# Two experts' halves of a shared K-tile as 64-row matmuls side by side, with outputs rotating over three PSUM banks

## The reference

```
hmid = gelu(einsum('tc,ech->eth', xf, w1) + b1, approximate=True)   # 4 experts, 576 hidden
eo = einsum('eth,ehc->etc', hmid, w2) + b2
moe = einsum('te,etc->tc', cw, eo)                                  # cw: top 2 of 4, softmax
x = x + g_mlp * moe
```

## Time and profile before

| | us |
|---|---|
| median of 3 runs | 472.41 |
| lowest and highest | 471.92, 477.0 |
| the profiled execution | 469.73 |
| its span, first to last instruction | 467.9 |
| PE busy | 416.6 |
| DVE, ACT, POOL busy | 281.4, 270.9, 129.5 |

### The profile page before, as it was taken

The page is one execution under the profiler, slowest core; times in us unless marked ns, Lnnn a source line. Parts: engine busy times, 40 slices in busy tenths (PEclk is TensorE's granted clock), DMA queues, the critical chain, the costliest instruction groups (busy, mean ns, idle before and its releaser), DMA issues.

```text
span 467.9 us, 10745 instructions
## 1 busy us (share of the span) xinstructions
PE 416.6 (89%) x4010; PEld 337.7 (72%) x4010; DVE 281.4 (60%) x797; ACT 270.9 (58%) x515; POOL 129.5 (28%) x214
## 2 busy tenths in 40 slices
PE   3784689898899999999998999998899998999997
PEld 1353568586676689878976897798678676768885
DVE  7965577687964426258623663257776657774642
ACT  4543277986596580382067336813677766777662
POOL 3104034352212072036008300714142432121000
PEclk9976599999999999999999999999799999999999
DMA  7955555546444000100010205203336465210212
GB/s 210 194 131 159 143 159 144 150 128 162 156 116 125 20 1 2 27 0 1 0 27 1 56 23 162 91 2 78 102 109 176 155 150 177 75 42 1 52 50 77
DMA packets 51570, 42.51 MB, mean 91 GB/s; under 512 B 33595, under 2 KB 43762, under 8 KB 51514
## 3 DMA queue, kind: packets, MB, share of 16 engines
q1 hardware_dynamic: 51450, 41.80, 32.7%
q10 hardware_dynamic: 68, 0.02, 0.0%
HBM read 33.20 MB, written 8.29 MB: 89 GB/s over the span
## 4 chain that ended last, share of the span: by engine, by line
PE 56%; DVE 13%; ACT 10%; SPq 7%; issue 6%; DMA 5%; POOL 3%; DVEq 0%; ACTq 0%; POOLq 0%
PE bank L1687 14%; PE bank L1705 4%; PE s_pair L1525 3%; PE bank L1567 3%; PE st_pair L1548 3%; DVE mx L1258 3%; PE s_pair L1465 2%; SPq L692 2%; PE s_pair L1472 2%; PE s_pair L1466 2%; PE s_pair L1469 2%; PE st_pair L1465 2%; PE bank L1458 2%; DMA hid<-mT 2%; PE st_pair L1466 2%
## 5 line engine op out<-in xcount | busy, mean ns | idle before, releaser
L1258 DVE TENSOR_REDUCE mx<-s_pair 128x8 f32<-128x1024 f32 x62 | 75.7, 1221 | 37.5 <-PE s_pair L1525 37.0
L961 ACT ACTIVATE pr<-st_pair 128x1024 f32<-128x1024 f32 x64 | 65.6, 1025 | 27.7 <-PE st_pair L1548 27.4
L1687 PE MATMUL bank<-w_sb,hid 128*128 128x144 f32 x640 | 80.5, 287 | 1.0 <-DVE aT L1337 1.0
L1687 PEld LDWEIGHTS bank<-w_sb,hid 128*128 128x128 f32 x640 | 79.6, 190 | 1.8 <-DVE aT L1337 1.2
L1010 ACT ACTIVATE hid<-s_pair 128x512 f32<-128x512 f32 x40 | 23.3, 612 | 51.5 <-PE s_pair L1472 51.4
L1567 PE MATMUL bank<-pr,V 128*10 128x128 f32 x1024 | 41.3, 280 | 0.0
L790 POOL TENSOR_TENSOR rstd<-var_eps,minus_half 128x4 f32<-128x4 f32 x16 | 16.6, 1035 | 77.1 <-DVE var_eps L1212 77.0
L1525 PE MATMUL s_pair<-KA,QA 81*128 81x128 bf16 x400 | 33.3, 231 | 4.4 <-DVE mx L1258 2.6
L1548 PE MATMUL st_pair<-QA,KA 83*128 83x128 bf16 x416 | 34.0, 228 | 2.4 <-DVE mx L1258 1.4
L829 POOL TENSOR_TENSOR xs<-xs,tmp 128x144 f32<-128x144 f32 x32 | 17.1, 533 | 64.5 <-DVE tmp L1279 39.9
L844 POOL TENSOR_TENSOR bw<-b_sb,cw 128x576 f32<-128x576 f32 x16 | 20.3, 1272 | 51.2 <-DVE cw L1320 51.2
(11 more groups left out here) (279 smaller groups left out, 953.3 us busy)
## 6 DMA issues: line engine op xcount, KB each, us to landing
QA<-qk_scratch SPq DMA_DIRECT2D x25, 324.0 KB
KA<-qk_scratch SPq DMA_DIRECT2D x75, 108.0 KB
qk_scratch<-parts SPq DMA_DIRECT2D x16, 288.0 KB, 4.0
g_att<-gate_scratch SPq DMA_DIRECT2D x16, 144.0 KB, 4.2
g_mlp<-gate_scratch SPq DMA_DIRECT2D x8, 288.0 KB, 3.7
hid<-qk_scratch SPq DMA_DIRECT2D x6, 324.0 KB
hid<-qk_scratch SPq DMA_DIRECT2D x18, 108.0 KB
qk_scratch<-parts SPq DMA_DIRECT2D x16, 96.0 KB, 3.3
```

Source lines behind the costliest of these rows:

```text
L961: sc.activation(pr[:, Pn % 2, :], st_pair[:, :], ACT.Exp, scale=SCALE).then_inc(s["exp_s"], 1)
L1258: v.tensor_reduce(mx[:, HP * h:HP * (h + 1)], src[:, :].rearrange("p (h k) -> p h k", k=SEQ), AX.X, ALU.max).then_inc(s["max_s"], 1)
L1687: last = te.matmul(dst, hid[:, at:at + SEQ], w2_sb[:, MT1 * e + i, :], start=(i == 0), stop=(i == MT1 - 1))
```

## The change

For the first three groups (batches t < 12):

- each expert's output goes to its own bank, in turn to banks 4, 5 and 7 by (4t + e) % 3 (`expert_out`), and PE waits for `acc_s` ahead of each expert, for the read of three outputs before, in place of once ahead of each pair;
- in the shared tile the even expert's call takes only rows 0 to 63 and the odd one's only rows 64 to 127, of both sides;
- since bank 7 is now used by both, `logits` waits until all the outputs of the groups before have been read, and the first pair of a group waits for `gate_s`, the gate's copy out of that bank.

Group 3 keeps its calls, banks and waits. `w2_mm` still counts pairs.

```diff
+        def expert_out(t, e):
+
+            if t < BATCH - G:
+                return DOWN_BANK[(EXPERTS * t + e) % 3][:, 0:C]
+            return bank[O_BANK[e // 2]][:, (e % 2) * C:(e % 2 + 1) * C]
...
-                    src = bank[O_BANK[e // 2]][:, (e % 2) * C:(e % 2 + 1) * C]
+                    src = expert_out(t, e)
...
                 need(pe, "mt_c", BATCH)
                 need(pe, "gate_s", 4 * g)
+                need(pe, "acc_s", EXPERTS * G * g)
...
                 if j == 0:
                     need(pe, "gelu", MT0 * g + MT0 // 2 * (pair + 1))
-                need(pe, "acc_s", 4 * t - 2 + 2 * pair)
+                if t >= BATCH - G:
+                    need(pe, "acc_s", 4 * t - 2 + 2 * pair)
+                elif j == 0:
+                    pe.wait_ge(s["gate_s"], 4 * g + 1)
                 for e in (2 * pair, 2 * pair + 1):
-                    dst = bank[O_BANK[pair]][:, (e % 2) * C:(e % 2 + 1) * C]
+                    if t < BATCH - G:
+                        need(pe, "acc_s", EXPERTS * t + e - 2)
                     for i in range(MT1):
                         at = (e * HID // P + i) * GT + j * SEQ
-                        last = te.matmul(dst, hid[:, at:at + SEQ], w2_sb[:, MT1 * e + i, :],
+                        half = t < BATCH - G and i == (MT1 - 1 if e % 2 == 0 else 0)
+                        k = slice(e % 2 * (P // 2), (e % 2 + 1) * (P // 2)) if half else slice(0, P)
+                        last = te.matmul(expert_out(t, e), hid[k, at:at + SEQ], w2_sb[k, MT1 * e + i, :],
                                          start=(i == 0), stop=(i == MT1 - 1))
                 last.then_inc(s["w2_mm"], 1)
```

## The result

| | before | after |
|---|---|---|
| median, us | 472.6 (4 runs) | 478.1 (4 runs, 477.13 to 480.04) |
| ratio after / before | | 1.0133, 95% interval 1.0098 to 1.0168 |
| profiled execution, us | 469.73 | 478.26 |
| span, us | 467.9 | 476.4 |

The change makes the kernel slower by 1.3%, 6.3 us with an interval of 4.6 to 7.9. The medians of the table are 5.5 us apart; the ratio leaves out executions of the kernel before that came out slower at a lower mean granted clock. The forecast was 477.4 us.

A forecast was written before the change was run, and what follows sets the result against it. PE, busy 89% of the span, was taken as the bound. Groups 0, 1 and 2 add 1.5 + 2.1 + 1.4 = +5.0 us to the 472.4 us median: 477.4 us, range 472.5 to 481.5.

The forecast's parts named there:

- The price of a pair: On PE, groups 0 to 2: two 93 ns drains, two 105 ns exposed loads, less 245 ns overlap: about +0.16 us.
- The bank wait: PE waits inside pairs for DVE's reads; with the pairs' price, groups 0, 1, 2 lose 1.5, 2.1, 1.4 us.
- The wait in group 1: Sign in the profile after: PE waits for DVE's reads inside pairs, over 1.5 us in group 1.
- What costs nothing: The logits' wait and the wait on `gate_s` are free; group 3 and the second layer keep their durations.
- Rival 3: Expert pairs, groups 0 to 2: 64-row halves do not drain, each pair gains 0.24 us; 470.8 us, chance 0.15.
- Rivals 1 and 2: Expert pairs: 1, poorer overlap, 0.25 or 0.28 us more, chance 0.15; 2, no overlap, 0.40 us more, chance 0.10.
- rival 2: Expert pairs, groups 0 to 2: no overlap, both switches, +0.40 us a pair, 2.85 us; 481.2 us, chance 0.10.

The follow-up runs named there:

- one stretch: Changed kernel, half calls in groups 0 and 1 only, on four banks, each batch's four half calls together: groups 0 and 1 take 19.14 and 20.05 us.
- the single half: Kernel before, with only the even or only the odd expert's call on 64 rows: pair 2.84 us; ratio 1.0156 for the even one.
- pairs rotate: Kernel before with full calls, both outputs of a pair in one bank, pairs rotating over three banks in groups 0 to 2: ratio 0.9967.
- the rotation alone: Changed kernel with its three-bank rotation and waits, but every call on all 128 rows: ratio 1.0005; groups +1.94 us over the kernel before.

## Why the prediction was right

**The price of a pair** was taken as +0.155 to 0.16 us and is +0.15 (2.60 us, against 2.45). Its terms stand one by one in the profile: a gap of 0.22 for 0.12 at each end (predicted 93 ns lost), records of 0.39 us (predicted), two of four slots gone. The assumption that carried most risk, that rows behave as columns do, both in overlap and in emptying, is confirmed by the stretch above. The step that made it possible was to find in the kernel before the one line, L1668, that used few rows and all columns.

By the Trainium skill's TensorEngine Tiling ("Key Properties"), changing the mode drains and changing the tile within it does not; "one stretch" agrees with both halves of the rule: 0.12 us between couples inside, once the first has loaded, and 0.22 at the ends.

**The bank wait.** Groups 0, 1 and 2 were put at +1.5, +2.1 and +1.4 (sum 5.0), and are +1.48, +1.94 and +1.39 (sum 4.8). The wait in group 1 was to be "over 1.5 us" and is 1.43, so this sign was missed by a little. The term that was a little off is group 1's: PE goes on 5.61 us into the group and its third pair starts at 7.14 us, both as worked out, but in the kernel before the matmul that waited until 217.06 had an exposed load as well, so its pair took 2.55 us and not 2.45. I had not counted that 0.1 us for the kernel before. The rest is the pair's own price, 0.01 lower each time.

**What costs nothing** held: the wait on `gate_s` and that of the logits appear in no list of PE's waits, the stretches between the groups are as long as before, and group 3 takes 24.61 us before and 24.62 after.

**The rivals.** Rival 3 (no drain) is out: pairs are longer, not shorter. Rivals 1 and 2 are out: 2.60 us and not 2.7 or 2.85; the 2.84 of the single half shows what rival 2 would have looked like.

**The sum and the whole.** The inner part gives +4.8 us, the ratio +6.3 us twice, where +5.0 was forecast. The intervals (4.6 to 7.9, 4.3 to 8.3) hold 4.8. The granted clock accounts for the rest. The profiled executions by stage (ahead of group 0, then the inner part; the number ahead of the last two is the mean granted clock), before and after:

```profile
0.00:171.10 171.10, 138.20 (x1515) 101.33 (x1516) 113.50 (x312) 109.46 (x211) 48.17 (x99) 0.92 0.51 137
171.10:299.73 128.63, 123.61 (x778) 107.42 (x776) 64.13 (x216) 59.89 (x115) 39.62 (x44) 1.00 0.13 35
...
0.00:175.47 175.47, 142.10 (x1515) 103.75 (x1516) 112.92 (x312) 109.52 (x211) 47.99 (x99) 0.90 0.49 133
175.47:308.93 133.46, 128.54 (x777) 105.14 (x776) 64.39 (x216) 59.89 (x115) 39.64 (x44) 1.00 0.11 34
```

The part ahead of group 0, where the code is the same, is 4.4 us longer in the profile after, at a lower mean clock. Over all profiles it lies between 170.4 us (clock 0.92) and 177.8 us (0.88, "pairs rotate", which is fast inside). The clock has two levels here, 2.4 and 1.2 GHz, so the mean clock and the span of an execution give its time at the lower one: 38.4 us on average in the 49 executions of the kernel before that have a clock on record, 42.7 us in the ten of the change. A straight line through both, an estimate, puts 0.38 us on each of these us, so 1.6 of the 6.3 us between their means, and leaves the change 4.7 us, give or take 0.8. That is the inner part's 4.8. The prediction added the groups' loss to the median before and said nothing of the clock: the groups lost 0.2 us less than it had, and the median still came out 0.7 us above the forecast. Whether the change itself brings about the longer time at the lower clock stays open; in the two profiles of the change none of it lies in the inner part.

## What to carry to other kernels

Count the switches of the array's division, not the idle rows: a call on 64 rows between full ones costs two emptyings and two exposed weight loads, 0.39 us here, and gives back only what runs beside it, 0.24 us for two fp32 calls of 144 columns side by side. Collect such calls into one stretch (four calls in a stretch were enough here, two were not), or leave the zeros in. And when outputs rotate over more banks, work out for each of them how much of PE's work lies between the read it needs and the write that waits: three banks with one output each were tighter here than two banks with two.

## What the runs showed of the hardware

- The step from no price to the full price lies between 65 and 64 rows (pair 2.45 against 2.84 us), and a half at row 64 costs what one at row 0 costs.
- Half-row loads of 128 columns take as long as full ones, 184 ns against 190, and two of them run at once: four are through in 0.30 us. L1567's loads of 10 columns on all rows take 92 ns. The Trainium skill's "TensorE: Matmul & The Clock Gate", under LDWEIGHTS, has the time go with the columns and not with the rows; the trace agrees.
- Both instructions of an fp32 call take part in the overlap: the four instructions of two calls start as two couples, 0.22 us apart on entering a stretch and 0.12 inside one. A wait between the two calls undoes the overlap (group 0's second pair, 2.85 us for 2.60).
- A matmul held up by a wait starts with an exposed load (0.39 us record for 0.29), so in a run of full calls each such wait costs some 0.1 us more than it shows. At a switch, where the load is exposed anyway, it does not: group 0 of the change lost 0.25 us to its wait, the rotation alone 0.37.
